# Half of each tile's attention probabilities turned through DRAM and by VectorE's 32x32 blocks in place of TensorE

## The reference

```python
x = x + attention(layernorm(x), ctx, ctx)      # inside: softmax over 77 keys per head, + residual, layer norm
x = x + moe(layernorm(x))                      # 4 of 32 experts per token, and one shared expert
```

## Time and profile before

| | |
|---|---|
| median of 3 runs | 856.4 us (855.65 to 857.94) |
| the profiled execution | 855.39 us, its span 853.6 us |
| PE busy | 772.0 us (90%) |
| DVE busy | 505.9 us (59%) |
| ACT busy | 444.5 us (52%) |
| POOL busy | 378.4 us (44%) |
| DMA | 164.38 MB, mean 193 GB/s |
| mean granted clock of PE | 0.968 |

### The profile page before, as it was taken

How to read it: one execution, slowest core, us unless ns; L and a number is a source line. 1 busy time by engine, 2 the same in 40 slices (tenths; PEclk the granted TensorE clock), 3 DMA queues, 4 the chain that set the end, 5 groups by cost and what they waited for, 6 DMA issues and landing times.

```text
span 853.6 us, 17128 instructions
## 1 busy us (share of the span) xinstructions
PE 772.0 (90%) x3742; PEld 586.5 (69%) x3743; DVE 505.9 (59%) x1499; ACT 444.5 (52%) x1828; POOL 378.4 (44%) x352
## 2 busy tenths in 40 slices
PE   6866999999999999999967849999999999999995
PEld 4655577777776767667745427887787877788554
DVE  1774236485959587776846544555555555555388
ACT  2445767776776768576713102555455555555110
POOL 1001332324756474747576162555555555555200
PEclk9989999999999999999998789999999999999999
DMA  7345223324443344499478386667676765555797
GB/s 249 99 138 170 87 86 119 112 88 135 162 157 134 134 155 140 165 292 362 161 245 313 111 292 217 191 214 221 193 223 200 229 207 179 166 180 159 278 408 333
DMA packets 104454, 164.38 MB, mean 193 GB/s; under 512 B 10885, under 2 KB 87763, under 8 KB 102867
## 3 DMA queue, kind: packets, MB, share of 16 engines
q1 hardware_dynamic: 90227, 120.02, 43.6%
q0 software_dynamic: 13824, 41.96, 13.4%
q10 hardware_dynamic: 352, 1.80, 0.6%
HBM read 90.01 MB, written 78.97 MB: 198 GB/s over the span
## 4 chain that ended last, share of the span: by engine, by line
PE 60%; DVE 10%; issue 9%; DMA 8%; ACT 5%; POOL 3%; SPq 2%; ACTq 2%; another core or an unknown queue 1%; DVEq 0%; POOLq 0%
PE psum L1639 13%; PE psum L1487 12%; PE psum L1522 11%; PE psum L1394 10%; PE psum L1653 6%; PE psum L1562 3%; DVE big L1357 3%; DMA big<-in_x 2%; ACT sm L828 2%; DMA xblk<-expert_lists 2%; POOL expert_lists L672 2%; PE psum L1577 2%; PE psum L1417 1%; DVE st L954 1%
## 5 line engine op out<-in xcount | busy, mean ns | idle before, releaser
L710 POOL DMA_INDIRECT y_d<-sm,yrow x160 | 155.4, 971 | 132.7 <-issue 91.3
L1639 PE MATMUL psum<-big,xbT 128*128 x640 | 166.5, 383 | 3.7 <-DVE xbT L1327 3.1
L672 POOL DMA_INDIRECT expert_lists<-rows,slot x128 | 127.1, 993 | 86.6 <-DVE slot L1171 47.9
L828 ACT ACTIVATE sm<-psum,nmax 128x77 f32<-128x77 f32 x512 | 157.6, 369 | 5.7 <-DVE nmax L1188 2.5
L1487 PE MATMUL psum<-big,xnT 128*128 (+2 forms) x384 | 143.0, 522 | 9.2 <-ACT sm L828 8.6
L1522 PE MATMUL psum<-big,pT 128*128 (+1 forms) x640 | 143.6, 379 | 0.0
L1522 PEld LDWEIGHTS psum<-big,pT 128*128 128x128 f32 x640 | 119.1, 190 | 14.9
L828 ACT ACTIVATION_READ_ACCUMULATOR sm<-psum,nmax 128x1 f32 x512 | 128.3, 251 | 0.0
L688 POOL TENSOR_TENSOR sm<-sm,sinv 128x1232 f32<-128x1232 f32 x32 | 72.0, 2249 | 125.6 <-DVE sinv L1225 125.4
L1639 PEld LDWEIGHTS psum<-big,xbT 128*128 128x128 f32 x640 | 109.1, 190 | 15.9 <-issue 7.4
L1487 PEld LDWEIGHTS psum<-big,xnT 128*128 128x128 f32 x384 | 71.2, 193 | 69.0 <-issue 52.8
(11 more groups left out here) (190 smaller groups left out, 1004.4 us busy)
## 6 DMA issues: line engine op xcount, KB each, us to landing
xblk<-expert_lists SPq DMA_DIRECT2D x160, 160.0 KB
y_d<-zero SPq DMA_DIRECT2D x32, 512.0 KB
big<-y_d SPq DMA_DIRECT2D x8, 2048.0 KB, 16.5
big<-in_L_ffn_W SPq DMA_DIRECT2D x16, 320.0 KB
xin<-in_x SPq DMA_DIRECT2D x36, 128.0 KB
big<-in_x SPq DMA_DIRECT2D x8, 512.0 KB, 3.5
xres<-in_x SPq DMA_DIRECT2D x8, 512.0 KB, 4.9
x_d<-x SPq DMA_DIRECT2D x8, 512.0 KB, 3.0
```

What stands on the lines that cost most here:

```text
L672: pool.indirect_dma_start(out=lists, out_offset=bass.IndirectOffsetOnAxis(ap=slot[:, ph, tt, k:k + 1], axis=0), in_=rows[:, ph, tt, :], in ...
L710: pool.indirect_dma_start(out=y_d, out_offset=bass.IndirectOffsetOnAxis(ap=yrow[:, q:q + 1], axis=0), in_=eo[:, q, :], in_offset=None).the ...
L828: last = nc.scalar.activation(sm[:, t % 2, h * SK:(h + 1) * SK], head_scores(h, h + 1), ACT.Exp, bias=nmax[:, t % 2, h:h + 1], accum_out=s ...
L1639: last = mm(bank(2 + q % 2)[:, 0:2 * H], xbT[:, q % 2, k, :], ew[:, bass.ds(e, 1), k * 2 * H:(k + 1) * 2 * H], start=k == 0, stop=k == KC - 1)
```

## The change

Of the ten blocks of 128 keys of a tile's probabilities, the first five (`DC` = 5, 640 columns) no longer go through PE and ACT. SP stores them from `sm` to DRAM (`p_d`), in 512 pieces of 640 bytes, each partition's row cut into four segments of 160. It loads them back into `by_seg`, a part of the large buffer, so that partition 32a + j holds segment a of tokens 4j to 4j+3 (128 rows of 2560 bytes). DVE then turns 32x32 blocks within each quarter of the partitions, one instruction for all 640 columns, into the first five blocks of `pT`. The keys in these blocks have an order of their own, so `VO` is made in the same order: its first five blocks are transposed from a strided view of `voT`. PE transposes the other five blocks, ACT copies them in two pieces, and PE's product takes these five first and then the turned ones. `by_seg` has one buffer; the load of a tile waits for the turn of the tile before.

SP's step gets this for tile n-2 between its load of x and its store of zeros. SP's loop over the middle groups is written out. In the last group SP's step comes ahead of `load_experts` and no longer behind it. `ln1g` and its copy are gone; ACT reads `ln1` at the tile's own place.

```diff
+            def turn_p(j, p, t):
+                m = num(j, p, t)
+                wait(sp, "probs_ready", m + 1)
+                wait(sp, "p_loaded", m * 16)
+                sp.dma_start(p_d[t % 2].rearrange("a r e -> r a e"),
+                             sm[:, t % 2, 0:4 * SEG].rearrange("p (a e) -> p a e", a=4)).then_inc(s["p_stored"], 16)
+                wait(sp, "p_stored", (m + 1) * 16)
+                wait(sp, "p_turned", m)
+                sp.dma_start(by_seg, p_d[t % 2].rearrange("a (j c) e -> (a j) (c e)", c=4)).then_inc(s["p_loaded"], 16)
...
                 if live(j, p):
                     wait(sp, "xn_ready", num(j, p, t) + 1)
                     load_x(jn, pn, t)
+                if live(*tile_ago(j, p, t, 2)[:2]):
+                    turn_p(*tile_ago(j, p, t, 2))
...
-            for p in range(2):
-                for t in range(TG):
-                    step(0, p, t)
-            with sp.Fori(1, NG // 2 - 1) as j:
+            for j in range(NG // 2 - 1):
...
             for t in range(TG):
+                step(NG // 2 - 1, 1, t)
                 load_experts(EARLY + (MIDDLE - EARLY) * t // TG, EARLY + (MIDDLE - EARLY) * (t + 1) // TG, "weights")
-                step(NG // 2 - 1, 1, t)
...
             def exp_scores(j, p, t):
                 n = num(j, p, t)
                 wait(act, "inverted", n - 1)
-                wait(act, "pt_psum", (n - 1) * 3)
+                wait(act, "pt_psum", (n - 1) * 2)
+                wait(act, "p_stored", (n - 1) * 16)
...
+                jm, pm, tm = tile_ago(j, p, t, 2)
+                if live(jm, pm):
+                    m = num(jm, pm, tm)
+                    wait(dve, "p_loaded", (m + 1) * 16)
+                    wait(dve, "out_psum", m - 1)
+                    nc.vector.transpose(pT[:, tm % 2, 0:DC, :].rearrange("p c (j r) -> p c r j", r=4),
+                                        by_seg.rearrange("p (r i c) -> p c r i", r=4, c=DC)).then_inc(s["p_turned"], 1)
...
-                if t == 1 and live(*ago(j, p, -1)) and live(j, p):
-                    group_ln1(*ago(j, p, -1))
...
-                    for c in range(CK):
-                        if c % 4 == 0:
-                            wait(pe, "pT_sbuf", m * 3 + (c // 4 + 1))
+                    for i in range(CK):
+                        c = (DC + i) % CK
+                        if c == 0:
+                            wait(pe, "p_turned", m + 1)
+                        elif c >= DC and i % 4 == 0:
+                            wait(pe, "pT_sbuf", m * 2 + (i // 4 + 1))
...
-                    for c in range(CK):
-                        last = transpose(pt_ps[:, c * P:(c + 1) * P], sm[:, tm % 2, c * P:(c + 1) * P])
+                    for c in range(PC):
+                        last = transpose(pt_ps[:, c * P:(c + 1) * P], sm[:, tm % 2, (DC + c) * P:(DC + c + 1) * P])
```

More of the change, by code:

```diff
@@ L76, in attention_moe_kernel @@
     RING = 4
+    DC = 5
+    PC, SEG = CK - DC, DC * P // 4
     assert BLOCKS % PE_TURN == 0 and PE_TURN % NX == 0 and BLOCKS % ACT_TURN == 0 and LAG <= PACK and E <= 256
@@ L1436, in product @@
                 p0_moved(pe, *[("vo", d, h) for h in range(NH)])
-                for i in range(min(4, CK - c)):
-                    last = transpose(ps[:, i * P:(i + 1) * P], voT[:, b, (c + i) * P:(c + i + 1) * P])
+                for i in range(c, min(c + 4, CK)):
+                    keys = (voT[:, b, i * P:(i + 1) * P] if i >= DC else
+                            voT[:, b, 0:DC * P].rearrange("p (n c) -> p c n", c=DC)[:, i, :])
+                    last = transpose(ps[:, (i - c) * P:(i - c + 1) * P], keys)
                 return last
@@ L1511, in step @@
                 if live(jn, pn) and live(j, p):
-                    wait(pe, "pT_sbuf", (n - 1) * 3)
+                    wait(pe, "pT_sbuf", (n - 1) * 2)
                     transpose_x(jn, pn, tn).then_inc(s["xt_psum"], 1)
```

46 lines of the change are left out of this document (22 added, 24 removed).

## The result

The changed kernel takes 880.8 us (median of 4 runs, 878.7 to 883.3) where the kernel before, run beside it, took 856.8 (855.7 to 857.9): a ratio of 1.027, 95% interval 1.023 to 1.030. It is slower by 24 us; 7 us less had been forecast. The profiled execution has a span of 876.6 us against 853.6. One kernel of the experiments, fast_turn, met a second, slower state in three of its four executions, the profiled one among them, so only its stretch up to tile 28 is used.

The account below looks back on a forecast made before the run. PE was taken as the bound (90% of the span), plus group pauses and full transfers in the last group. 855.4 -12.5 -4 +1 +0.5 +8 = 848.4, median 1.0 above: 849.4; own range 841 to 857, overall 834 to 867.

Parts of the forecast that it names:

- Five transposes fewer, -12.5: Attention stage up to tile 28: five PE transposes fewer save 0.545 us per tile, 12.5 us taken between 10.9 and 14.2.
- The estimate of 36 us: Attention stage: alternative saving for five fewer transposes, at about 275 ns each, 1.4 us a tile; the trace disagreed.
- The turn on VectorE, +1: Each tile's turn on VectorE, 0.83 us, stays mostly hidden: 1 us lost in all, bounds 0 to 6.
- C: Rival: the turn takes 2.8 us or is blocked by POOL, making VectorE the bound in two steps per group; 863, chance 0.1.
- The pauses, -4: Three slow groups: breaking up SP's burst of four transfers shortens PE's pauses, 4 us gained, bounds 8 gained to 6 lost.
- The round trip in quiet groups, 0: Store and load of probabilities before the last group, 3.0 us each, fit the slack of 4.0 and 1.4 us: no cost.
- Before the stage, +0.5: Ahead of the attention stage, 40 transposes of folded values read with a stride of five: 0.5 us lost, bounds 0 to 6.
- The last group, +8: Tiles 28 to 31: SP's round with weights and awaited store takes 14 us; stage ends 8.0 us later, bounds 0 to 17.
- Rival B: Last group: stores behind weights end it 17 to 20 us later, pauses stay, 10.9 us gained; 866, chance 0.17.
- What follows "shifts whole": Behind the last group, routing, tables and list fills are one chain and shift whole, with no further term.
- Wrong: PE waits for the turn from the first tiles on: Attention stage: PE waiting for the turn from the first tiles on was named as a sign against the forecast.
- the group of over 46 us: Groups of four tiles: one taking over 46 us was a sign against the forecast; slow groups were expected at 41 to 44.

Follow-up runs that it names:

- fast_turn: The changed kernel with VectorE's turn contiguous in and out for every tile (half the result meaningless): 864.3 us in one execution, kernel before 859.2.
- five_only: The changed kernel without the DRAM round trip and VectorE's turn (half the probabilities left out): 824.2 us, kernel before 824.8, ratio 0.997.
- traffic_only: The changed kernel with all ten blocks turned by PE, no VectorE turn, store and load kept: 836.9 us, kernel before 824.8, ratio 1.014.
- no_transfers: The changed kernel with VectorE's turn but without store and load of probabilities (half left out): 841.4 us, kernel before 824.8, ratio 1.019.
- fast_first_order: The changed kernel with the turn contiguous and ahead of the maxima, and the last group's weights ahead of SP's step: 845.2 us, ratio 1.025.
- five_order: five_only with the last group's expert weights issued ahead of SP's step, as in the kernel before: 846.9 us, kernel before 859.2, ratio 0.988.
- before_again: The kernel before, unchanged, run again for its trace on another chip: 858.0 us, kernel before beside it 859.2.
- before_w_late: The kernel before with the last group's expert weights issued behind the last step: 834.8 us, kernel before 825.2, ratio 1.011.
- after_again: The changed kernel, run again on another chip beside parts of it: 852.7 us, kernel before 824.8, ratio 1.033.
- w_late: The changed kernel with the last group's expert weights issued behind the last step's load: 846.0 us, kernel before 825.2, ratio 1.025.
- turn_views: The changed kernel with VectorE's turn read and written in four ways, strided or contiguous, by tile in group: 850.4 us, kernel before 825.2.
- after: The changed kernel itself in the first comparison and its profile: 880.8 us, kernel before 856.8, ratio 1.027.
- pool_queue: The changed kernel with store and load of probabilities issued by POOL instead of SP: 890.4 us, kernel before 861.1, ratio 1.039.

## Why the prediction was wrong

The forecast was 31 us below the result, 30 in the profiled executions. By stretches of the profiled executions, against the kernel before: up to tile 28 it had 15.5 us gained and 1.7 were (13.8 off), in the last group 8 lost and 17.4 were (9.4 off), behind the last product nothing and 9.4 were lost, before tile 0 it had 0.5 lost and 2.2 were gained. The step that failed most is the price of the turn on VectorE, and the next is the size of the last group. By its own steps, in its order:

- **Five transposes fewer, -12.5.** Right in mechanism and nearly in size: -10.7 us up to tile 28 (five_only against traffic_only), all in three of a group's four steps. Even steps of 9.22 us came as forecast. The estimate of 36 us from the figure of the Trainium skill ("TensorE: Matmul & The Clock Gate", Part 4: PE-mode transpose) would have been far off.
- **The turn on VectorE, +1.** This is the step that failed: 17.2 us by no_transfers against five_only (18.6 up to tile 28), where 6 was the upper bound. Two errors. Its length was 1.37 us, not 0.83; the forecast took an elementwise row as the nearest and looked at the number of columns, not at the steps of 20 and 16 bytes between them. And the slack was counted for one instruction in one step. The earlier trace rows showed VectorE waiting 0.43 us ahead of the fourth tile's maxima, which is what the third step's work left, and I let ACT's reserve swallow the rest; but work that is late in the third step is still late in the fourth, and a turn stands in front of the step's other work in each. The size follows from the windows: without the turn VectorE has 9.3 us to do in a third step of 9.9. With 1.37 more that is 10.7 (measured 10.6), and the step becomes 11.3. Of the rivals, C had the place right and the cause wrong (a turn of 2.8 us or one blocked by POOL; no turn of the changed kernel took more than 1.43). Even a turn of 0.83 us would not have been free: up to tile 28 fast_turn stays 11 us above five_only and fast_first_order, with the turn ahead of the maxima, 5 us.
- **The pauses, -4.** On the first chip they did go: no scores of a second or third tile wait as in the earlier trace rows. In five_order, beside before_again, the slow groups fall from 44.9 to 46.3 us down to 41.0, 20 us up to tile 28; 10.7 of it are the transposes, by the pair on the other chip, which leaves 9 for the pauses. So the gain was larger than forecast, and in the changed kernel the turn took it all. That SP's burst of four transfers caused the pauses is not shown; on the faster chips even the kernel with the old SP order (before_w_late) has none.
- **The round trip in quiet groups, 0.** Right: up to tile 28, 23 of 27 stores land in 2.5 to 3.2 us (the others in 3.5 to 7.4, the last of them behind the shared expert's activations), VectorE waits for none of the loads before tile 28, and the transfers cost 0.4 us up to there.
- **Before the stage, +0.5.** Not to be measured: tile 0's first score comes at 75.2 us instead of 77.4, but among traces of the same code it comes at 74.9 to 78.6. The 80 transposes take 10.7 us against 11.9.
- **The last group, +8.** Right mechanism (SP's chain: weights, load of x, a store that is waited for), too small: +17.4 on the first chip, 12.8 of that by the transfers' own comparison. The tile's 9.5 us on PE were misread, since the 38.04 us of the earlier trace rows are not four steps but three (35.1 us) and 2.9 us; the sum does not use them. The forecast starts the weights with tile 28; they start 3.4 us later (373.46 against 370.03), since a step of SP stands ahead of them now. From weights to weights the three rounds take 12.2, 15.6 and 16.5 us instead of 12.8, 14.0 and 14.0, 3.7 in all (weights 6.8 to 7.5 in place of 6.2, the store 5.6 to 6.4 in place of 5.4). The forecast also had no term for what a waiting PE does afterwards: three times ten matmuls mostly at the lower clock, some 2 us more each, of which one stands at the end of the chain. Together, tile 30's product ends 68.7 us behind tile 28's first score instead of 59.7. And the forecast assumed that a faster kernel meets the last group's other work as it was; five_only shows that 8.8 us are lost there without any transfer of p, 6 of them by the order that the change swapped. Rival B had the size (+19) and came nearest to the whole: 866. Its mistake was to keep 10.9 us of gain, which is the turn again. (Rival C's 863 is 1.4 less than its own "+15 on the forecast" gives.)
- **What follows "shifts whole".** Not on the first chip: 7.3 us more from the last product to the first expert. On two other chips the changed kernel has 67.3 us there, its parts 66.7 to 67.1. On the slower chips this stretch goes from 85.6 to 92.9 us among all kernels without late weights, 88.7 in the kernel before on its second chip, so some of the 7.3 belongs to the run. What made the rest is open, and so are the 2.1 us more behind it.
- **Traces of failure named beforehand.** "Wrong: PE waits for the turn from the first tiles on" is what happened from the eighth tile on, and the group of over 46 us was nearly reached (45.75; 46.4 in after_again).

No version here that moves half of the probabilities to VectorE and computes the whole result beats the kernel before. The nearest, w_late, is 2.5% behind it; fast_first_order, whose turned half is in another order, is too. Faster are only kernels that leave half of the probabilities out, five_order by 1.2%.

## What to carry to other kernels

Work that is moved to an engine with idle time on average costs its full length wherever that engine's own order is nearly full, and the backlog can carry over into the next step: read the busy time of the receiving engine step by step, in windows, before pricing it at nothing. Price an operation by its strides as well as by its columns. And a kernel that is made faster in the middle meets the transfers at its end sooner: here the last group took back 9 of 11 us from the kernel that only had less to do, 6 of them by a side edit of the order.

## What the runs showed of the hardware

- VectorE's 32x32 turn of 128x640 fp32: 0.83 to 0.85 us contiguous on both sides, 1.31 to 1.43 with a stride of 16 or 20 bytes on either or both (turn_views, fast_turn, after).
- The store of 320 KB lands mostly in 2.5 to 3.2 us from SP and in 3.0 to 4.2 from POOL with little beside it, and in 5.6 to 6.4 (after) and 6.2 to 7.0 (pool_queue) beside the weights. The turn that waits for the load back starts 2.7 to 3.4 us behind its issue on SP (after), and 3.2 to 6.2 on POOL (pool_queue). POOL's two issues take 0.82 and 0.56 us.
- TensorE's granted clock is 1.00 ahead of a wait of 2.15 us and 0.61 behind it, 0.55 behind one of 5.47 us, and ten matmuls take 4.1 to 4.3 us instead of 2.3 (after).
- The same kernel differs by 4% between chips (825 and 857 to 861 us). The changed kernel's traces differ by 25.6 us in the stretch from the last product to the first expert (92.9 against 67.3) and by under 1 us up to tile 28. The kernel before was not traced on a faster chip; by its variant before_w_late it has 8 us less of pauses up to tile 28 there, and by the other kernels 19 to 22 us less between the last product and the first expert. The pauses can be won only where there are any.
